# A DeltaNet layer with a Hadamard FFN on one core: the first and last rounds of pairs in written-out orders, and the gate chain ahead of the FFN fold

## The reference

```
S = S * exp(g_t);  delta = (v_t - k_t S) * beta_t;  S = S + k_t^T delta;  o_t = q_t S
```

## Time and profile before

| what | value |
|---|---|
| median of 3 runs | 899.07 us (896.51 to 902.03) |
| the profiled execution | 898.49 us |
| its span | 896.7 us |
| TensorE matmul busy | 805.4 us (90%), 12586 instructions |
| VectorE busy | 702.2 us (78%) |
| ScalarE / Pool busy | 324.7 (36%) / 273.0 us (30%) |
| DMA, mean | 55 GB/s |

### The profile page before, as it was taken

How to read it: one execution, slowest core, us unless ns; L and a number is a source line. 1 busy time by engine, 2 the same in 40 slices (tenths; PEclk the granted TensorE clock), 3 DMA queues, 4 the chain that set the end, 5 groups by cost and what they waited for, 6 DMA issues and landing times.

```text
span 896.7 us, 29194 instructions
## 1 busy us (share of the span) xinstructions
PE 805.4 (90%) x12586; PEld 550.7 (61%) x12586; DVE 702.2 (78%) x1208; ACT 324.7 (36%) x737; POOL 273.0 (30%) x186
## 2 busy tenths in 40 slices
PE   1837689999999999999999999999999999998775
PEld 1414356666766677666666677666666666667664
DVE  4945868888897979888898979897888889795622
ACT  2303525243444335252434344343525234443110
POOL 3004231615142332516150423333161615143110
PEclk9969989999999999999999999999999999999787
DMA  8022131413123131313131131313131313111101
GB/s 231 22 58 48 36 78 38 89 39 76 39 46 71 32 66 55 67 37 78 38 88 39 31 85 34 70 42 64 40 85 39 78 37 78 26 27 19 24 4 47
DMA packets 129151, 49.34 MB, mean 55 GB/s; under 512 B 110976, under 2 KB 120576, under 8 KB 128896
## 3 DMA queue, kind: packets, MB, share of 16 engines
q1 hardware_dynamic: 128400, 47.34, 23.5%
q10 hardware_dynamic: 624, 0.15, 0.1%
HBM read 39.85 MB, written 7.60 MB: 53 GB/s over the span
## 4 chain that ended last, share of the span: by engine, by line
PE 66%; DVE 20%; DMA 5%; SPq 3%; issue 3%; ACT 2%; POOL 0%; POOLq 0%; DVEq 0%; ACTq 0%
PE bank L587 19%; DVE kq L224 7%; PE bank L599 6%; PE bank L643 6%; PE bank L751 5%; PE bank L667 4%; PE bank L662 3%; PE bank L753 3%; PE bank L695 3%; PE bank L723 3%; PE bank L706 3%; PE bank L681 2%; PE bank L606 2%; SPq L525 2%; PE bank L671 2%
## 5 line engine op out<-in xcount | busy, mean ns | idle before, releaser
L587 PE MATMUL bank<-xnT,wq 128*128 128x512 f32 x512 | 253.7, 620 | 21.0 <-DVE kq L224 20.8
L224 DVE SCALAR_TENSOR_TENSOR kq<-bank,cw,kq 128x510 f32<-128x510 f32 (+2 forms) x288 | 214.4, 745 | 18.3 <-ACT kq L802 11.1
L587 PEld LDWEIGHTS bank<-xnT,wq 128*128 128x128 f32 x512 | 89.0, 193 | 94.9 <-issue 66.1
L950 POOL TENSOR_TENSOR kqg<-kq,rows 128x1024 f32<-128x1024 f32 x32 | 76.4, 2388 | 176.1 <-issue 108.2
L802 ACT ACTIVATE kq<-bank,cw 128x512 f32<-128x512 f32 x96 | 65.7, 685 | 150.4 <-issue 66.6
L956 POOL TENSOR_TENSOR Sd<-St,dec 128x256 f32<-128x256 f32 x32 | 19.9, 622 | 299.9 <-DVE St L339 205.4
L751 PE MATMUL bank<-wo,oT 128*128 128x256 f32 x256 | 74.6, 395 | 2.2 <-DVE oT L363 1.6
L960 POOL TENSOR_TENSOR ost<-ost,cst 128x8 f32<-128x8 f32 x32 | 52.4, 1636 | 64.7 <-DVE ost L351 63.2
L643 PE MATMUL bank<-kq 64*64 64x128 f32 x1024 | 69.2, 273 | 0.9 <-DVE ATP L270 0.9
L270 DVE TENSOR_TENSOR ATP<-bank,gb 128x512 f32<-128x512 f32 x64 | 44.1, 689 | 32.6 <-PE bank L643 30.5
L723 PE MATMUL bank<-d,ATP 64*64 64x64 f32 x1024 | 67.5, 230 | 1.5
(11 more groups left out here) (129 smaller groups left out, 1334.7 us busy)
## 6 DMA issues: line engine op xcount, KB each, us to landing
rows<-decay_rows SPq DMA_DIRECT2D x64, 256.0 KB, 4.5
wq<-wqkvz_dram SPq DMA_DIRECT2D x16, 512.0 KB, 3.8
inverse_blocks<-UU SPq DMA_DIRECT2D x16, 256.0 KB, 2.0
wguT<-wgu_dram SPq DMA_DIRECT2D x8, 256.0 KB, 3.0
woraw<-wout_dram SPq DMA_DIRECT2D x16, 128.0 KB, 2.3
base_blocks<-ATP SPq DMA_DIRECT2D x128, 16.0 KB, 1.8
UU<-base_blocks SPq DMA_DIRECT2D x16, 128.0 KB, 2.0
U<-inverse_blocks SPq DMA_DIRECT2D x128, 16.0 KB, 1.9
```

The source lines that it names most:

```text
L224: nc.vector.scalar_tensor_tensor(out=y[:, :, t:S], in0=p[:, :, 0:S - t], scalar=cw[:, m, i // 2, 3 - t:4 - t], in1=y[:, :, t:S], op0=ALU.m ...
L587: last = nc.tensor.matmul(ring[i % 2][:], wq[:, q, kc, i // 2, :], xnT[:, kc, (i % 2) * 512:(i % 2) * 512 + 512], start=kc == 0, stop=kc = ...
L950: nc.gpsimd.tensor_tensor(kqg[:, q, :, half(H)].rearrange("p k u c -> p k (u c)"), src, g, ALU.mult).then_inc(kqg_done, 1)
```

## The change

1. `program` takes three lists: a head, the order of a full round and a tail. The head holds everything of rounds up to 3 and the tail everything from round 11 on, each step with its pair's number, for VectorE, SyncE, TensorE, ScalarE and Pool; rounds 4 to 10 run the same order as before. The steps are the same ones; head and tail put many of them one to six places earlier or later.
2. In the setup on VectorE the variance stands ahead of `wscaled(0)`, one of the first two butterflies goes behind the copies of xnT and `coef`, the four late butterflies and beta go behind `rows_made`.
3. The four fold matmuls go from the end of TensorE's setup into its third projection of pair 0, behind the transposes of the rows; ScalarE's four copies into its third tap of pair 0. The first gram of pair 0 awaits them (`wd_used`).

```
+        def program(do, head, order, tail):
+            def run(m, step):
+                name, *number = step.split(".")
+                do[name](m, m % 2, *map(int, number))
+            for step in head.split():
+                m, step = step.split(".", 1)
+                run(int(m), step)
+            for n in range(4, 11):
+                for step in order.split():
+                    kind, step = step.split(".", 1)
+                    run(n + ahead[kind], step)
+            for step in tail.split():
+                m, step = step.split(".", 1)
+                run(int(m), step)
...
+                dve.wait_ge(sq_done, TT)
+                step(nc.vector.tensor_scalar(st[:, 0, :], st[:, 2, :], 1.0 / HID, LN_EPS, ALU.mult, ALU.add))
+                steps["var"] = count[0]
                 dve.wait_ge(wdn_in, 16)
                 dve.wait_ge(wsd_in, 16)
                 wscaled(0)
-                dve.wait_ge(sq_done, TT)
-                step(nc.vector.tensor_scalar(st[:, 0, :], st[:, 2, :], 1.0 / HID, LN_EPS, ALU.mult, ALU.add))
-                steps["var"] = count[0]
                 wscaled(1)
...
+                butterfly(wds[1], wds[0], 1, 0)
                 for q in (1, 3):
-                    butterfly(wds[1], wds[0], 1, q // 2)
...
-                for t in range(2):
-                    butterfly(wds[0], wds[1], 2, t)
-                for t in range(2):
-                    butterfly(wds[1], wds[0], 4, t)
-                steps["fold"] = count[0]
-
+                butterfly(wds[1], wds[0], 1, 1)
                 dve.wait_ge(ba_ready, 1)
...
-                step(nc.vector.tensor_scalar(ga[:, 0, :, :], ga[:, 4, :, :], -1.0, -1.0, ALU.mult, ALU.add))
-                step(nc.vector.reciprocal(beta[:], ga[:, 0, :, :]))
...
                 dve.sem_inc(rows_made, 1)
+                step(nc.vector.tensor_scalar(ga[:, 0, :, :], ga[:, 4, :, :], -1.0, -1.0, ALU.mult, ALU.add))
+                step(nc.vector.reciprocal(beta[:], ga[:, 0, :, :]))
+
+                for t in range(2):
+                    butterfly(wds[0], wds[1], 2, t)
+                for t in range(2):
+                    butterfly(wds[1], wds[0], 4, t)
+                steps["fold"] = count[0]
```

TensorE's and ScalarE's parts of the fold:

```
                         last.then_inc(rows_ready, 1)
+                        pe.wait_ge(v_step, steps["fold"])
+                        pe.wait_ge(xh_done, 4)
+                        for n in range(4):
+                            nc.tensor.matmul((CH, Z, TR, GR)[n][:], k("had"), wds[0][:, 2 * n:2 * n + 2, :], start=True, stop=True).then_inc(wd_ready, 1)
...
+                    if m == 0 and b == 0:
+                        pe.wait_ge(wd_used, 4)
...
+                            if m == 0:
+                                for n in range(4):
+                                    act.wait_ge(wd_ready, n + 1)
+                                    nc.scalar.activation(wdf[:, 4 * n:4 * n + 4, :], (CH, Z, TR, GR)[n][:].rearrange("p (t d) -> p t d", t=4), ACT.Copy,
+                                                         scale=1.0 / float(np.sqrt(INTER))).then_inc(wd_used, 1)
```

The beginnings of the heads (VectorE, TensorE, ScalarE, Pool, SyncE):

```
+0.proj.0 0.proj.1 0.e 0.proj.2 0.proj.3 0.proj.4 0.stats 0.proj.5 0.gram.0 0.gram.1 0.vtr.0 0.gram.2 0.ff 0.gram.3 1.e
+1.proj.0 1.proj.1 1.proj.2 0.inv.0 1.proj.3 0.inv.1 0.inv.2 1.proj.4 1.proj.5 1.stats 1.gram.0 1.ff 0.vtr.1 1.gram.1
+1.gram.2 0.hz.1.0 1.vtr.0 0.hz.1.1 0.hz.2.0 2.e 0.hz.2.1 0.hz.3.0 0.hz.3.1 1.gram.3 2.proj.0 0.state.0 2.proj.1 0.ks.1
...
+0.proj.0 0.proj.1 0.proj.2 0.proj.3 0.ktr.0 0.proj.4 0.ktr.1 0.proj.5 0.proj.6 0.gram.0 0.vtr.0 0.proj.7 0.gram.1
+0.vtr.1 0.ff 0.gram.2 0.gram.3 1.proj.0 1.proj.1 0.qsq 1.proj.2 1.proj.3 1.proj.4 1.proj.5 1.ktr.0 1.ktr.1 1.gram.0
+1.proj.6 1.proj.7 1.vtr.0 1.ff 1.gram.1 0.hz.0.0 0.hz.0.1 1.gram.2 0.hz.1.0 1.vtr.1 0.hz.1.1 0.hz.2.0 0.hz.2.1 1.gram.3
+0.hz.3.0 2.proj.0 0.hz.3.1 2.proj.1 0.delta.0 0.state.0 2.proj.2 0.ks.1 1.qsq 2.proj.3 0.delta.1 0.state.1 0.o.0.0
...
+0.proj.0 0.proj.1 0.proj.2 0.proj.3 0.ktr.0 0.dec 0.proj.4 0.ktr.1 0.proj.5 0.proj.6 0.vtr.0 0.oload 0.proj.7 0.ff
+0.qsq 1.proj.0 1.dec 0.vtr.1 1.proj.1 1.proj.2 0.qsum 1.proj.3 1.ktr.0 1.proj.4 0.inv.2 1.proj.5 1.ktr.1 1.proj.6
...
+0.kqg.0 0.root 0.gb.0 0.kqg.1 0.gb.1 0.kd.0 1.kqg.0 0.kd.1 1.kd.0 1.gb.0 1.gb.1 1.kqg.1 1.root 0.sd.1 0.sd.2 0.norm.0
...
+0.rload 0.fload 1.rload 0.bout 0.load 0.bin 1.fload 1.load 0.uout 0.uin 2.load 0.oload 2.rload 2.fload 1.bout 1.oload
...
```

The ends of the tails (VectorE, TensorE, Pool):

```
+13.gated.1 13.out.0 13.turn.1 14.vtr.0 13.out.1 14.vtr.1 13.out.2 15.stats 15.gram.0 13.out.3 15.gram.1 15.vtr.0
+14.hz.1.0 15.gram.2 14.hz.1.1 14.hz.2.0 15.gram.3 14.hz.2.1 14.hz.3.0 14.hz.3.1 14.state.0 14.ks.1 15.inv.0 14.state.1
+15.inv.1 14.ks.2 14.norm.0 14.state.2 14.ks.3 14.gated.0 15.inv.2 14.turn.0 14.norm.1 15.ff 14.gated.1 14.out.0
...
+15.gram.1 14.hz.0.0 14.hz.0.1 15.gram.2 14.hz.1.0 14.hz.1.1 14.hz.2.0 15.gram.3 14.hz.2.1 15.vtr.1 14.hz.3.0 14.hz.3.1
+14.delta.0 14.state.0 14.ks.1 14.delta.1 14.state.1 14.o.0.0 14.ks.2 14.o.0.1 14.delta.2 14.state.2 14.ks.3 14.delta.3
+14.o.1.0 14.turn.0 14.o.1.1 14.out.0 14.turn.1 14.out.1 14.out.2 14.out.3 15.qsq 15.hz.0.0 15.hz.0.1 15.hz.1.0
+15.hz.1.1 15.hz.2.0 15.hz.2.1 15.hz.3.0 15.hz.3.1 15.delta.0 15.state.0 15.ks.1 15.delta.1 15.o.0.0 15.state.1 15.o.0.1
+15.ks.2 15.delta.2 15.state.2 15.ks.3 15.turn.0 15.delta.3 15.o.1.0 15.o.1.1 15.out.0 15.turn.1 15.out.1 15.out.2
...
+14.kqg.0 14.kqg.1 14.kd.0 14.gb.0 14.gb.1 14.kd.1 14.root 13.sd.1 13.norm.0 13.sd.2 13.norm.1 15.kqg.0 15.gb.0 15.gb.1
+15.kd.0 15.root 15.kd.1 14.sd.1 15.kqg.1 14.sd.2 14.norm.0 14.norm.1 15.sd.1 15.sd.2 15.norm.0 15.norm.1
```

More of the change, by code:

```diff
@@ L777, in _ @@
                     last.then_inc(xh_ready, 1)
-                pe.wait_ge(v_step, steps["fold"])
-                for m in range(4):
-                    pe.wait_ge(xh_done, m + 1)
-                    nc.tensor.matmul(spare[m][:], k("had"), wds[0][:, 2 * m:2 * m + 2, :], start=True, stop=True).then_inc(wd_ready, 1)
                 program({"proj": proj, "ff": ff, "ktr": ktr, "vtr": vtr, "qsq": qsq, "gram": gram, "hz": hz, "ks": ks, "delta": delta,
-                         "state": state, "o": o, "turn": turn, "out": out}, """K.hz.3.1 M.proj.1 K.delta.0 L.vtr.1 K.state.0 M.proj.2 K.ks.1 L.qsq K.delta.1 M.proj.3 K.state.1 K.o.0.0 K.ks.2 K.o.0.1
+                         "state": state, "o": o, "turn": turn, "out": out}, """0.proj.0 0.proj.1 0.proj.2 0.proj.3 0.ktr.0 0.proj.4 0.ktr.1 0.proj.5 0.proj.6 0.gram.0 0.vtr.0 0.proj.7 0.gram.1
@@ L788, in _ @@
+                         15.hz.1.1 15.hz.2.0 15.hz.2.1 15.hz.3.0 15.hz.3.1 15.delta.0 15.state.0 15.ks.1 15.delta.1 15.o.0.0 15.state.1 15.o.0.1
+                         15.ks.2 15.delta.2 15.state.2 15.ks.3 15.turn.0 15.delta.3 15.o.1.0 15.o.1.1 15.out.0 15.turn.1 15.out.1 15.out.2
+                         15.out.3""")
             @block.scalar
```

95 lines of the change are left out of this document (77 added, 18 removed).

## The result

The changed kernel takes 909.96 us (median of 4, 906.54 to 917.00); the kernel before, on the same chip, 900.55. Ratio 1.0118 [1.0073, 1.0164]: slower by 1.2%, where 889.3 and faster was forecast. The profiled execution took 911.69 us, its span 909.9, against 898.49 and 896.7. TensorE's 12586 matmuls are the same.

What follows compares the result with a forecast made beforehand. TensorE bounds the full rounds, a setup chain the start, VectorE the filling. Terms of -9.5 (setup and filling), -1.5 (rounds) and +1.8 (end) sum to -9.2 on 896.7: 887.5, plus 1.8 around it, 889.3 us; range 882.5 to 895.5.

Steps and rivals of the forecast that it cites:

- What bounds the kernel: Full rounds: TensorE busy 668.3 of 682.2 us, one us idle per round, so orders can win little there.
- The setup, -7.2 at the third projection's taps: Setup: pair 0's third projection reaches VectorE at 56.2 instead of 63.40 us.
- gate product: Setup on VectorE: taken at 27.2 instead of 30.17 us, since it no longer waits for the fold.
- Layer norm: Setup: starts at 17.2 instead of 17.44 us, Pool's power and both scalings competing; 15.7 if they don't.
- Root against stats, +2.7: First rounds: Pool's root and a VectorE stats product of two SBUF operands exclude each other, costing 2.7 us.
- inv.0 against kqg, +2.2: First rounds: VectorE's inv.0 products stand behind Pool's kqg of pair 1, costing 2.2 us.
- Filling, -9.5 at pair 2's second projection: First rounds: TensorE reaches pair 2's second projection 9.5 us earlier, between 8.0 and 11 (128.5 or 125.5 against 136.49).
- Rounds 2 and 3, within -1.5: Rounds 2, 3 and 11 to 15: same work, -1.5 us for all seven, between -5 and +4.
- Rounds 11 to 15: Tail rounds: covered by the same -1.5 us for all seven rewritten rounds, between -5 and +4.
- The end, +1.8: From pair 15's gram.3 on: 1.8 us longer, 0 to +4, or -2 if the clock stays up.
- The signs of being wrong: Wrong if the first round's taps start later than 58 us, or any rewritten round passes 50 us.
- the slower one: Seven rewritten full rounds: fixed inversions add a 1.2 us wait in each, 8.4 us, giving 901.0; chance 0.06.

Runs made afterwards that it cites:

- mid_copies: mid_head with ScalarE's four copies of the fold ahead of its wait for pair 0's third projection: 894.59 us, ratio 0.9925 to the kernel before.
- setup_head: The changed kernel with its tail put back to the order of before: 906.31 us, ratio 1.0075 to the kernel before.
- setup_tail: setup_only with the changed kernel's written tail: 897.22 us, ratio 0.9963 to the kernel before.
- pool_kqg: setup_head with `2.proj.0` between pair 0's hz.1.0 and hz.1.1, and on Pool both kqg of pair 3 ahead of its gb.0: 906.67 us, 1.0041.
- mid_head: Changed kernel, rounds from 3 on in old order, SyncE's `1.oload` ahead of `1.bout`, TensorE's `2.proj.0` between hz.1.0 and hz.1.1: 897.05 us, 0.9971.
- setup_only: The changed kernel with only the setup changed, head and tail in the order of before: 897.20 us, ratio 0.9968 to the kernel before.

## Why the prediction was wrong

- **What bounds the kernel**: right. TensorE's full rounds have one us to spare, and rounds 4 to 10 came out unchanged. I used it as "orders can win little there"; it says as strongly that they can lose much, since each uncovered wait shows in full.
- **The setup, -7.2 at the third projection's taps**: 59.62 instead of 63.40, -3.8. Two terms failed. The copies: I counted a tap of 0.7 behind the projection and took the copies as running beside the fold matmuls; in the code they stand inside ScalarE's `proj`, behind its wait for the projection. mid_copies shows the step (56.80, forecast 56.2). The other is chance: the gate matmuls took 6.09 us in this execution and 3.94 in others of the same code (setup_head, setup_tail), so the gate product came at 28.24 where 27.2 was forecast and 26.0 in those. In nine of the twenty profiles they took 3.9 us, in the other eleven 5.7 to 7.0, whatever the orders. Layer norm came at 16.08, against 17.2: the power stood behind the first scaling alone, not behind both (see below). Rows at 41.30 (40.6), fold matmuls at half clock: as forecast. In runs the whole setup is -2.9 us, with the copies put right -6.0.
- **Root against stats, +2.7**: failed. Beside Pool's power the two products took 0.17 and 0.18 us. **inv.0 against kqg, +2.2**: right, 2.32 us for a product of 128x8. (Undisturbed, the two 64-element products of the earlier trace rows take 0.56 us, as at 98.76 in the changed kernel, and not the 0.91 that the prediction set against 2.60.)
- **Why the two differ.** By the rule of the Trainium skill ("SBUF — State Buffer", Who interferes with whom) both would have been held; the rows agree for Pool's products of two tiles and not for its power, once it runs. But the power can itself be held at its start. In twelve profiles Pool's power in the setup started ahead of VectorE's first scaling and took 1.64 us, as the later ones of the earlier trace rows do; in the other eight the scaling was already running, and it took 2.60 to 2.72. The scalings took 1.22 or 1.23 in all twenty. So the prediction's reading of the earlier trace rows, that Pool stood about 1.1 us behind VectorE, was right, and wrong only in that the second scaling was not in the way too, nor the power in that of root's neighbours. The start of mid_copies:

```profile
13.24 1.64 POOL L1059 TENSOR_TENSOR st<-st,cst 128x8 f32<-128x8 f32 x1 [7.78 <-DVE st L406]
13.32 2.48 DVE L403 TENSOR_TENSOR kqg<-kqg,wsd 128x1024 f32<-128x1024 f32 x2 [0.23 <-DMA kqg<-wdown_dram]
```

- **Filling, -9.5 at pair 2's second projection**: -1.8. The inverse left at 106.28 instead of 112.76 (103.3 was forecast) and pair 1's ff came 6.8 us earlier; then 2.32 us went in the gap, 1.7 in the lower clock behind it (granted 0.71 from 127.3 to 131.8 us, 0.92 up to 137), 0.7 in vtr.1, which stands ahead of delta now. None of these was in my walk: it followed VectorE, and I had moved TensorE's projection from between the small matmuls without asking what it did there.
- **Rounds 2 and 3, within -1.5**: +13.7 in the profile, and the step that cost the forecast. What I had at nothing was the hand-over between steps: a state behind its delta waits 0.48 us for ScalarE's copy, a turn or out 0.5 to 1.3 us for VectorE, wherever the step that stood between them is gone. By runs round 3 is 8 us, half of it the chain's waits, half the hand-over to the full rounds (the 1.8 us of pool_kqg, Pool's gb.0 ahead of kqg, would be part of that). Round 2 costs nothing by its order; behind the written filling it takes back 4 us of the lead, whichever of the two orders it has. That second fact fails the sum by itself: the forecast carried -9.5 us of setup and filling to the end, and by runs only -2.6 us arrive there with the written filling and round 2 (mid_head, 0.9971), no more than the -2.9 of the setup alone (setup_only, 0.9968).
- **Rounds 11 to 15**: +2.3 in the profile, 4 us in two pairs of runs out of three, each at the edge of what is told apart. **The end, +1.8**: -1.5 in the profile. o.0 ahead of state, ks ahead of gated cost nothing; out.1 behind turn.1 neither.
- **The signs of being wrong**: both came. The third projection's taps start at 59.62, later than 58, and the three rewritten stretches take 52.3, 56.3 and 51.1 us, more than 50.
- **The rivals**: the slower one had the right kind of mechanism, waits that lost their cover in rounds with one us to spare, and the wrong price and place: 1.2 us per round in all seven, where it is 8 in one of the head's and 0 to 4 in the tail's. Its chance of 0.06 rested on "each moved step stays within one or two places", which looks at the distance of a step and not at what stood between two steps that wait for each other.

By runs the sum is: setup -2.9; head +9.6 (round 3 +8, gap +1, filling and round 2 nothing); tail +3.9; together 10.6 us, the 1.0118. Of these the head's loss is beyond doubt and the setup's gain clear; the tail's 3.9 is known to 5 us only.

## What to carry to other kernels

In a list written by hand, look at the pairs of steps that wait on another engine (delta and state, turn and out) and at what stood between them: on an engine with one us of idle per round that filler is the schedule. Follow buffers as well as values: a step moved behind another on a side engine (kqg on Pool) can release a load later, which comes down on a far step. And a moved block of copies belongs ahead of the wait of the step that it is put into.
